# Layer 1's last token tile: sums by distance transposed earlier, three output tiles closed ahead of the fourth, four result buffers

## What is computed

```
xn  = layernorm(x)
qkv = xn' @ W_in.T + b_in                  # 16 heads of 64; attention runs over 8 positions, per token row
attn = softmax(q k + q k_dist[dist])       # dist = min(|t - s|, 10)
o    = attn v + sum_t attn v_dist[dist]    # the second term: weights summed by distance, times v_dist
s    = o @ W_out.T + b_out
g    = silu(sqrt((xn @ cos(theta + theta_noise))^2 + (xn @ sin(phi + phi_noise))^2))
x    = x + s * g
```

## Time and profile before

| | us |
|---|---|
| median of 3 runs | 1199.06 |
| lowest, highest | 1198.33, 1204.83 |
| the profiled execution, its own time | 1198.4 |
| its span (first to last instruction) | 1196.6 |
| PE busy | 1155.2 (97%) |
| DVE busy | 903.2 (75%) |
| ACT busy | 678.4 (57%) |
| POOL busy | 568.3 (47%) |

### The profile page before, as it was taken

How to read it: one execution, slowest core, us unless ns; L and a number is a source line. 1 busy time by engine, 2 the same in 40 slices (tenths; PEclk the granted TensorE clock), 3 DMA queues, 4 the chain that set the end, 5 groups by cost and what they waited for, 6 DMA issues and landing times. The chain is left out here.

```text
span 1196.6 us, 34938 instructions
## 1 busy us (share of the span) xinstructions
PE 1155.2 (97%) x14327; PEld 752.2 (63%) x14327; DVE 903.2 (75%) x2003; ACT 678.4 (57%) x1302; POOL 568.3 (47%) x589
## 2 busy tenths in 40 slices
PE   6899999999999999999989999999999999999997
PEld 5434444444444444443368797878879787887976
DVE  7876887878787887878275877678697767769766
ACT  4457776776777677767643444445354544535453
POOL 2157685877868586777522303132240413224031
PEclk8689999999999999999999999999999999999999
DMA  8545253553625355452240010010101001010100
GB/s 245 122 100 126 73 133 108 117 152 81 158 65 135 96 120 129 98 153 72 72 128 1 4 54 4 15 42 4 54 5 53 4 15 42 3 55 4 36 4 19
DMA packets 57998, 86.80 MB, mean 73 GB/s; under 512 B 8304, under 2 KB 38256, under 8 KB 57840
## 3 DMA queue, kind: packets, MB, share of 16 engines
q1 hardware_dynamic: 57680, 84.31, 26.7%
q10 hardware_dynamic: 160, 0.26, 0.1%
HBM read 50.40 MB, written 33.55 MB: 70 GB/s over the span
## 5 line engine op out<-in xcount | busy, mean ns | idle before, releaser
L1122 DVE TENSOR_REDUCE negmax<-s_bank 128x1 f32<-128x512 f32 x512 | 330.3, 679 | 69.7 <-PE s_bank L765 69.1
L1317 POOL TENSOR_TENSOR room<-room 128x512 f32<-128x512 f32 x248 | 311.0, 1287 | 116.4 <-ACT room L932 116.4
L932 ACT ACTIVATE room<-t_bank 128x512 f32<-128x512 f32 x512 | 284.2, 600 | 81.6 <-PE t_bank L775 78.3
L775 PE MATMUL t_bank<-qst,kst 50*128 50x512 f32 x512 | 200.4, 467 | 6.2 <-ACT room L932 5.9
L765 PE MATMUL s_bank<-kst,qst 48*128 48x512 f32 x512 | 192.4, 467 | 5.1 <-DVE negmax L1122 2.8
L775 PEld LDWEIGHTS t_bank<-qst,kst 50*128 50x128 f32 x512 | 81.0, 187 | 101.6 <-ACT room L932 62.7
L2082 POOL TENSOR_TENSOR win<-rt,apart 128x512 f32<-128x512 f32 x32 | 41.9, 1330 | 210.4 <-DVE rt L1890 210.4
L1612 PE MATMUL pr<-xt_h,win_h 128*128 128x512 f32 x256 | 105.9, 414 | 0.0
L2069 POOL TENSOR_TENSOR ex<-ex,rc 128x256 f32<-128x256 f32 x64 | 41.7, 652 | 131.6 <-DVE rc L1918 131.3
L1612 PE MATMUL pr<-xt_h,win_l 128*128 128x512 f32 x256 | 100.5, 393 | 0.0
L1612 PE MATMUL pr<-xt_l,win_h 128*128 128x512 f32 x256 | 100.5, 393 | 0.0
(11 more groups left out here) (337 smaller groups left out, 2567.9 us busy)
## 6 DMA issues: line engine op xcount, KB each, us to landing
park<-qk_h SPq DMA_DIRECT2D x126, 128.0 KB, 2.4
qst<-park SPq DMA_DIRECT2D x64, 192.0 KB, 3.3
kst<-park SPq DMA_DIRECT2D x64, 192.0 KB, 4.2
park<-qk_l SPq DMA_DIRECT2D x64, 128.0 KB, 2.4
room<-in_x SPq DMA_DIRECT2D x8, 512.0 KB, 5.4
xr<-in_x SPq DMA_DIRECT2D x8, 512.0 KB, 6.2
room<-x SPq DMA_DIRECT2D x8, 512.0 KB, 3.9
out<-so SPq DMA_DIRECT2D x32, 128.0 KB, 1.7
```

What stands on the lines that cost most here:

```text
L775: pe.matmul(t_bank[w % 2][:, :], kst[slot][rows, j, c * P:(c + 1) * P], qst[slot][rows, j, :], start=True, stop=True).then_inc(m.t_done, 1)
L932: act.activation(probs[:, c, j, :], t_bank[w % 2][:, :], ACT.Exp, scale=SCALE0).then_inc(m.exp_done, 1)
L1122: dve.tensor_reduce(negmax[:, i_par, 2 * odd + j, c:c + 1], s_bank[n % S_BANKS][:, :], X, ALU.max, negate=True).then_inc(m.max_done, 1)
L1317: add = pool.tensor_tensor(sums[:, pair, h, :], probs[:, 2 * pair, h, :], probs[:, 2 * pair + 1, h, :], ALU.add)
```

## The change

It alters the last tile (i = 7) of layer 1 alone. For the other tiles the same instructions are issued in the same order.

- PE: the four transposes of `pd` stand ahead of block 0's outputs; blocks 1 and 2 are closed after the first half of block 0's outputs; block 0 is closed after its second half; then come block 3's 24 matmuls in one piece, and its closing matmul. No matmul is added or taken away. `pdt_ok` is waited for ahead of each of the three closings.
- DVE: n = 0 and 1 together, then n = 2 alone, then n = 3 alone. The results go to four buffers, `xn[:, n, :]`, in place of `so[n % 2]`, so the waits for `stored` at n = 2 and 3 are dropped.
- SP: stores from the four buffers, in the same order, with the same semaphores.

```diff
+        def so_at(i, n):
+
+            return xn[:, n, :] if i == NT1 - 1 else so[:, n % 2, :]
...
-                    sp.dma_start(o_rows[i, W_ORDER[t]], so[:, t % 2, :]).then_inc(m.stored[t % 2], 16)
+                    sp.dma_start(o_rows[i, W_ORDER[t]], so_at(i, t)).then_inc(m.stored[t % 2], 16)
...
+                def by_distance():
+                    pe.wait_ge(m.pd_ok, 2 * (i + 1))
+                    misc_free()
+                    for u in range(TT):
+                        mm = pe.transpose(misc[:, u * P:(u + 1) * P], pd[:, u, :, :].rearrange("p h r -> p (h r)"),
+                                          ident[:, :])
+                    mm.then_inc(m.pd_psum, 1)
+                    prev_misc[0] = ("PD", i, 0)
+
+                def finish(tiles):
+                    pe.wait_ge(m.pdt_ok, i + 1)
+                    for t in tiles:
+                        pe.matmul(w_bank(t)[:, 0:E], pdt[:, t * P:(t + 1) * P], ud[:, :],
+                                  start=False, stop=True).then_inc(m.w_psum, 1)
+
+                if last:
+                    by_distance()
+                    outputs(0, range(HP // 2))
+                    finish(W_ORDER[:2])
+                    outputs(0, range(HP // 2, HP))
+                    finish(W_ORDER[2:3])
+                    outputs(3, range(HP))
+                    finish(W_ORDER[3:])
+                else:
+                    outputs(0, range(HP))
+                    by_distance()
+                    outputs(3, range(HP // 2))
                     transposes(i + 1, 1)
...
+                    outputs(3, range(HP // 2, HP))
+                    finish(W_ORDER)
...
                 if n < 2:
                     wait(dve, m.stored[n], 16 * 2 * i)
-                else:
+                elif i < NT1 - 1:
                     dve.wait_ge(m.stored[n % 2], 16 * (2 * i + 1))
...
-                for n in (0, 2):
-                    read_output(i, n)
-                    read_output(i, n + 1)
-                    gate_output(i, n)
-                    gate_output(i, n + 1)
+                for group in ((0, 1), (2,), (3,)) if last else ((0, 1), (2, 3)):
+                    for n in group:
+                        read_output(i, n)
+                    for n in group:
+                        gate_output(i, n)
```

More of the change, by code:

```diff
@@ L1745, in body @@
                 wait(pe, m.so_ok, TT * i)
[L1746 to L1754, removed]
-                    transposes(i + 1, 1)
[L1756 to L1760, removed]
+                def by_distance():
[23 more added lines that the diff above has]
+                    outputs(3, range(HP // 2))
+                    transposes(i + 1, 1)
+                    outputs(3, range(HP // 2, HP))
+                    finish(W_ORDER)
             over_batches(body)
@@ L1978, in read_output @@
                         o_ps[:, 0, :])[t]
-                dve.tensor_tensor(so[:, n % 2, :], bank[:, 0:E], bout[:, :], ALU.add).then_inc(m.so_ok, 1)
+                dve.tensor_tensor(so_at(i, n), bank[:, 0:E], bout[:, :], ALU.add).then_inc(m.so_ok, 1)
             def gate_output(i, n):
@@ L1984, in gate_output @@
                 dve.wait_ge(m.so_ok, TT * i + n + 1)
-                dve.scalar_tensor_tensor(so[:, n % 2, :], so[:, n % 2, :], 0.5, q2[:, t, :], op0=ALU.mult,
+                dve.scalar_tensor_tensor(so_at(i, n), so_at(i, n), 0.5, q2[:, t, :], op0=ALU.mult,
                                          op1=ALU.mult).then_inc(m.sg_ok, 1)
@@ L1989, in gate_output @@
                     dve.wait_ge(m.xr_load, 16 * (i + 1))
-                dve.tensor_tensor(so[:, n % 2, :], so[:, n % 2, :], xr[:, t, :], ALU.add).then_inc(m.x2_ok, 1)
+                dve.tensor_tensor(so_at(i, n), so_at(i, n), xr[:, t, :], ALU.add).then_inc(m.x2_ok, 1)
             norm_stats(0)
```

## The result

| | before | after |
|---|---|---|
| median, us | 1202.7 (22 runs) | 1198.49 (22 runs) |
| lowest, highest | 1198.33, 1206.62 | 1194.99, 1203.34 |
| ratio to before, 95% interval | | 0.9969 [0.9956, 0.9982] |
| profiled execution: time, span | 1198.4, 1196.6 | 1198.68, 1196.8 |

The change makes the kernel 0.31% faster, 3.7 us of 1202.7; the interval runs from 2.2 to 5.3 us, and the two medians lie 4.2 us apart. I had forecast -3.5 us, and no difference larger than 0.5%; both came so. But I had written the time down from a base of 1198.4 to 1199.1, since the three runs of before that were shown had a median of 1199.06. Over 22 runs the kernel before has 1202.7. So 1198.49 lies above my 1195.2, and 0.3 us outside the range.

The account below looks back on a forecast made before the run. PE was taken as the bound until its last matmul, then DVE and one store; tail -3.65 and PE +0.16 gave -3.49 us. From 1198.4 and 1199.06 this gave 1195.2 us, range 1193.9 to 1198.2.

Parts of the forecast that it names:

- What bounds the kernel: PE until its last matmul, then DVE and one store; only 5.2 us ahead of the last store's issue can be reached.
- The cost of two more returns from float32, 0.16 us: Last tile on PE: each of two new switches from float32 back to fp32r costs 0.08 us.
- starts 0.20 us apart: Sign on PE in the changed profile: starts 0.20 instead of 0.12 us apart once behind each float32 piece.
- The moved waits on PE: Last tile: `pd` is ready 1.12 us before PE asks, ACT's copy of `pdt` 0.64 us before; both waits hidden.
- DVE: Last tile: earlier results are covered by PE; n = 3 starts 0.09 us after PE, ends at 1190.86, store issued at 1190.96.
- The sum: Last store's issue moves by -3.49 us: exposed tail shrinks from 5.2 to 1.5 us, -3.65, and PE pays +0.16.
- The base: Whole-kernel time the gain is taken from: profiled 1198.4 gives 1194.9, median 1199.06 gives 1195.6; 1195.2 taken between.
- rival 1: More lost at PE's switches and waits in the last tile: gain only 2.2 us, time 1196.5; 12%.
- (1) to (3): Rivals: more lost at PE's switches, 12%; stores still hold the tail, about 1198.4 to 1199, 3%; late `pd_ok`, slower, 1%.
- (3): Slower: late `pd_ok` stalls PE ahead of block 0; price is lateness minus 1.12 us, 1199.8 at 6 us; 1%.
- (4): The clock: PE is granted 1.00 at the end and the change adds no gap; no case of its own, no chance given.
- the span 3.5 us shorter: Sign in the changed kernel's profile: the whole span falls by 3.5 us to 1193.1.

Follow-up runs that it names:

- the variant with two: Against the change with two operations behind the last closing: distance terms of blocks 0 and 3 added where blocks 1 and 2 are closed; ratio to before 0.9995.
- the kernel with the filled gap: The change plus 11 unused 128x512 matmuls in PE's idle gap at 24.2 us in layer 0; ratio to before 0.9981, median 1201.47 us.
- the kernel with the filled maxima: The change plus 10 unused matmuls in layer 0's 24.2 us gap and one ahead of each of the next 21 score matmuls; ratio to before 1.0099.

## Why the prediction was right or wrong, point by point

**What bounds the kernel.** Right. The tail behind PE's last matmul was all that the change could reach, and PE's own last stretch kept its 13.87 us.

**The cost of two more returns from float32, 0.16 us.** Wrong: nothing, shown twice (13.87 us before with one return and in the change with three, 13.88 in the variant with two). I had read 0.08 from the gap of 0.20 between the first and second fp32r matmul behind the transposes. But four transposes at 0.107 a step are 0.43 us, and from 1184.08 that is 1184.51; the first fp32r record starts early, at 1184.43, overlapping them, and its successor keeps its own distance of 0.12 to the true end. The early start and the late successor are one thing. For the transposes my 0.35 + 0.08 was their whole cost; behind the closings I took the whole 0.87 and added 0.08 again. The sign that I named, starts 0.20 us apart, came behind the transposes and was 0.31 behind the closings (1187.69 to 1188.00), and still cost nothing: 1187.02 + 0.87 + 0.12 = 1188.01.

**The moved waits on PE.** Right: no idle time of PE ahead of the transposes or of a closing. ACT's copy of `pdt` started at 1185.78, 6.42 us after the first output matmul; expected 1181.83 - 1175.42 = 6.41.

**DVE.** Right to 0.2 us. Shifted by 3.94, n = 0 was expected at 1187.70 and started at 1187.71; n = 2 at 1190.09, 1190.01. The two dependent steps took 0.46 each (1193.25, 1193.71, 1194.17), close to the 0.45 of the earlier trace rows and not 0.34. The last issue was expected at 1190.96 + 3.94 = 1194.90 and came at 1194.68; the 0.22 us are the returns (0.16) and a start behind the last closing after 0.02 where I had taken 0.09. One of the earlier stores I had misread: n = 0 was issued at 1189.39, which is 1185.45 on the clock of the prediction and not about 1185.8; it is off the path.

**The sum.** -3.49 us forecast; -3.74 in the last stretch, and 0.31% of 1202.7, 3.7 us, over 22 runs each. The split into removed waits and earlier closings was not in my sum, and the runs give it: the order alone is worth all of it, the buffers 1.6 alone and nothing with it. I named "there are only two result buffers" as a part of what the change removes; it was so for the old order only.

**The base.** This is the step that failed. I took 1195.2 from 1198.4 and 1199.06, and treated the third run, 1204.83, as an outlier with 6% for a median that high. Three runs with a gap of 6 us between them were in fact samples of a wide spread: 1198.33 to 1206.62 over 22, with its middle at 1202.7. The trace shown pointed to its origin. In the page's slices of 30 us the granted clock is below full in the first three (0.89, 0.67, 0.87) and 0.94 in one between the layers, 600 to 630 us; in layer 0 there are stretches at 0.50, and a single profile can't say how long these are in other executions. Had I put the sum on the middle of the three's range, (1198.33 + 1204.83) / 2 = 1201.6, it would have given 1198.1, 0.4 us from the result; so close a hit would have been luck, but the range would have reached the result. The range of 1193.9 to 1198.2 went only 1.7 us beyond the 1196.5 of rival 1 to allow for the spread, while the base that 1195.2 stands on, 1198.7, was 4.0 us too low.

**The rivals.** (1) to (3) did not occur. The price of (3) was added to the profiled 1198.4, not to the base of the sum: from 1195.2 a lateness of 6 us would give 1195.2 + 6 - 1.12 = 1200.1, not 1199.8. Of my signs, the span 3.5 us shorter did not come (1196.8 where I had 1193.1), by the base's failure again and not by the mechanism's. For (4) I wrote that the clock was no case: true of the last stretch, and blind to layer 0, where it moves the whole run by more than the change is worth.

**Open.** What brings on the stretches at 1.2 GHz in layer 0, and why they differ between executions of one kernel, isn't settled. That they go with lost time is shown by marks and by the runs' clocks. That the idle gap alone brings on the one from 24 us was tried and fell; that it has a part in how long it lasts was not excluded.

## What to carry to other kernels

When work is closed in parts, let all parts but one finish under the cover of the engine that is the bound; then only the last part's chain counts, and buffers that were scarce behind the bound engine can stop to matter. Compare a small change by a stretch with a mark at its beginning, not by whole spans: the last stretch of the change was 17.44 to 17.53 us in the four profiles that share it, while runs of one kernel differed by 8 to 13 us. And before a small difference is put on a base, ask how wide the base is: three runs with a 6 us gap between them are a spread, not a value and an outlier.

## What the runs showed of the hardware that I had not expected

- The granted clock stood at 0.50 for 3 us at a time with PE busy in all 3.00 of them (24 to 27 us in the kernel with the filled gap). PE had run 32 matmuls of 16 columns (L730, 19.6 to 23.3 us) just before. The same 32 stood ahead of the filled gap in the kernel with the filled maxima, where the clock then was 1.00, so they don't settle it.
- A 128-row matmul of 512 columns costs 0.23 us a step in a row of its kind and 0.43 when it alternates with 48-row ones, at the same granted clock of 1.00. The weight loads aren't hidden there; whether the row count or the waits between them are the reason was not tried.
- Going from float32 matmuls to fp32r ones cost nothing: the first one's record starts early, 0.08 us ahead of the end of four transposes and 0.20 ahead of that of two closings (1187.69 against 1187.89), and the next keeps the true distance of 0.12.
